# A four-block graph network on one core: x W1 between the counting windows, degrees from a column of ones, and the normalization moved from the matrix to rows and sums

## The reference

```python
ones = jnp.ones((src.shape[0],), x.dtype)
deg = jax.ops.segment_sum(ones, dst, num_segments=num_nodes) + 1.0
inv = jax.lax.rsqrt(deg)
h = x @ W
norm = inv[src] * inv[dst]
agg = jax.ops.segment_sum(h[src] * norm[:, None], dst, num_segments=num_nodes)
agg = agg + h * (inv * inv)[:, None]
return agg + b                       # then relu
```

## Time and profile before

| what | value |
|---|---|
| median of 3 runs | 5089.91 us |
| profiled execution | 5089.79 us |
| its span | 5087.7 us |
| TensorE busy in the span | 4957.9 us |
| counting | from 18.4 to 310.9 us |
| from the last count's copy to the first matmul of convolution 1 | 311.6 to 375.2 us |
| convolution 1, transposes, x W2, convolution 2, GRU inputs | 375.2 to 694.7 us |
| GRU and the three later blocks | from 698.9 us on |

### The profile page before, as it was taken

The page is one execution under the profiler, slowest core; times in us unless marked ns, Lnnn a source line. Parts: engine busy times, 40 slices in busy tenths (PEclk is TensorE's granted clock), DMA queues, the critical chain, the costliest instruction groups (busy, mean ns, idle before and its releaser), DMA issues.

```text
span 5087.7 us, 337016 instructions
## 1 busy us (share of the span) xinstructions
PE 4957.9 (97%) x131794; PEld 4250.1 (84%) x131795; DVE 2880.4 (57%) x16350; ACT 1950.7 (38%) x15372; POOL 846.6 (17%) x5071
## 2 busy tenths in 40 slices
PE   7899999999999999999999999999999999999989
PEld 7765579999999999999999999999999445555554
DVE  6551346666666666666666666666666525445551
ACT  0111025555555555555555555555555101222110
POOL 0000012222222222222222222222222000000000
PEclk9999999999999999999999999999999998999989
DMA  1011210000000000000000000000000100011011
GB/s 61 0 70 68 102 38 0 0 0 0 0 0 0 0 0 0 0 0 0 0 0 0 0 0 0 0 0 0 0 0 0 59 17 19 18 36 36 22 51 42
DMA packets 28932, 81.11 MB, mean 16 GB/s; under 512 B 1594, under 2 KB 1834, under 8 KB 28858
## 3 DMA queue, kind: packets, MB, share of 16 engines
q1 hardware_dynamic: 28858, 80.03, 4.3%
HBM read 58.08 MB, written 21.95 MB: 16 GB/s over the span
## 4 chain that ended last, share of the span: by engine, by line
PE 94%; DVE 2%; issue 2%; DVEq 1%; ACT 0%; POOL 0%; DMA 0%; ACTq 0%; SPq 0%; POOLq 0%
PE psum L494 64%; PE psum L567 8%; PE psum L363 5%; PE psum L353 4%; PE psum L579 4%; PE psum L411 3%; PE psum L476 2%; PE psum L553 2%; PE psum L643 2%; DVE r L880 1%; PE psum L426 0%; PE psum L458 0%; DVEq L875 0%; DVE r L879 0%; DVE stat L813 0%
## 5 line engine op out<-in xcount | busy, mean ns | idle before, releaser
L494 PE MATMUL psum<-h,r 128*128 128x16 f16 (+1 forms) x80000 | 3063.3, 181 | 9.1 <-ACT psum L707 4.3
L494 PEld LDWEIGHTS psum<-h,r 128*128 128x128 f16 x80000 | 2670.6, 96 | 39.1 <-DVEq L993 4.9
L494 PE MATMUL psum<-h,hn 128*128 128x16 f16 (+1 forms) x40000 | 2122.2, 177 | 0.0
L494 PEld LDWEIGHTS psum<-h,hn 128*128 128x128 f16 x40000 | 1592.6, 96 | 0.0
L999 DVE TENSOR_TENSOR_SCAN psum<-mul_rz,psum 128x6 f32<-128x6 f32 x5000 | 854.9, 171 | 590.8 <-PE psum L494 542.5
L707 ACT COPY psum<-big 128x2 f32 (+1 forms) x7506 | 1002.8, 163 | 0.0
L315 POOL TENSOR_TENSOR upd_add<-upd,signs 128x4 f32<-128x4 f32 x2500 | 504.2, 202 | 2591.2 <-DVE upd L1018 1832.0
L720 ACT ACTIVATE mul_n<-psum 128x2 f32<-128x2 f32 x2500 | 434.4, 174 | 1177.9 <-DVE psum L999 1177.8
L1018 DVE TENSOR_TENSOR_SCAN upd<-upd_mul,upd_add 128x8 f32<-128x8 f32 x2500 | 417.2, 167 | 300.4 <-ACT upd_mul L725 300.4
L729 ACT ACTIVATE upd_add<-psum 128x2 f32<-128x2 f32 x2500 | 434.1, 174 | 297.4 <-DVE psum L1005 297.4
L1014 DVE TENSOR_TENSOR_SCAN h<-upd_mul,upd_add 128x8 f16<-128x8 f32 x2500 | 425.2, 170 | 169.9 <-POOL upd_add L315 3.8
(11 more groups left out here) (224 smaller groups left out, 2538.1 us busy)
## 6 DMA issues: line engine op xcount, KB each, us to landing
ws<-in_Wl SPq DMA_DIRECT2D x9, 1024.0 KB, 5.4
ws<-in_Wr SPq DMA_DIRECT2D x9, 1024.0 KB, 7.6
edge_counts<-adj SPq DMA_DIRECT2D x2, 3051.8 KB
edge_weights<-big SPq DMA_DIRECT2D x1, 6103.5 KB
adj_rows<-big SPq DMA_DIRECT2D x1, 6103.5 KB
adj<-adj_rows SPq DMA_DIRECT2D x1, 6103.5 KB
big<-edge_counts SPq DMA_DIRECT2D x1, 6103.5 KB
adj<-edge_weights SPq DMA_DIRECT2D x1, 6103.5 KB
```

Source lines behind the costliest of these rows:

```text
L494: m = mm(places, whh16[g][:, part, 2 * kc + k, (2 * c + j) * P:(2 * c + j + 1) * P], state.unsqueeze(1).broadcast_to([P, COPIES, 2 - part] ...
```

## The change

- **x W1 in the counting.** `h1_half` puts two of the four matmuls of one tile of x W1 before each window. In 24 windows (12 rounds, H1 = NW // 2) that is 12 products for 10 tiles: two are computed twice. ScalarE stages the tile's columns of `r1` in `x_stage`, and copies each product from PSUM bank 4 to `hn`. `rows_product("h1", ...)` is gone. Before the first window TensorE now waits for W1. The edge columns `e_col` and `w_part` move out of `hn`.
- **Degrees from a column of ones.** `src_hot` holds 1 in column 1250 and 0 in columns 1251 to 1253, and VectorE writes only 1250 columns. So partition 125 of the tenth tile of the counts is the number of edges of each column. The windows are copied with 128 partitions. Ten matmuls with one column of the identity turn that row to a column; the 30 matmuls with ones and the ten of L435 are gone. Ten matmuls spread 1/max(degree, 1), ten more spread the inverse root.
- **No norm pass.** VectorE adds 1 on the diagonal only. ScalarE multiplies the rows of x W1 by `inv_col` (in place) and those of x W2 as it copies them. VectorE multiplies each sum of the convolutions by `inv_row` (`scale_cols`), and only then ScalarE adds bias and relu in place (`shift_cols`). The copies of the transposes become multiplications by `inv_col` and `inv_row`.
- **The counts in five stores** of 250 columns each, each issued when its five windows are copied.

```diff
+            for q in range(NW // 5):
+                sp.wait_ge(s("win_counts"), 5 * q + 5)
+                columns = slice(5 * q * WD, (5 * q + 5) * WD)
+                sp.dma_start(tiles(d_cnt)[:, :, columns], adj_v[0:NP, :, columns]).then_inc(s(f"cnt_out{5 * q // (NW - 5)}"), 16)
...
+            def h1_half(i, u):
+                if u == 0:
+                    pe.wait_ge(s("x_staged"), i + 1)
+                    pe.wait_ge(s("h1_stored"), i + 1)
+                for k in range(2 * u, 2 * u + 2):
+                    m = mm(psum[0:NP, 4], x_stage[:, k], wslot(0)[:, k], start=(k == 0), stop=(k == KT - 1), skip_group_check=True)
+                if u == 1:
+                    m.then_inc(s("h1_done"), 1)
...
+            pe.wait_ge(s("w1_in"), 16)
+            with pe.Fori(0, H1) as i:
                 for u in range(2):
+                    h1_half(i, u)
                     window(2 * i + u, u)
...
             pe.wait_ge(s("win_counts"), NW)
+            for t in range(NT):
+                m = mm(psum[0:NP, 7, t:t + 1], adj_v[:, NT - 1, t * NP:(t + 1) * NP], ident[:, NP:NP + 1], start=True, stop=True, skip_group_check=True)
+            m.then_inc(s("deg"), 1)
+            pe.wait_ge(s("win_read"), NW + 2)
+            pe.wait_ge(s("h1_stored"), H1 + 1)
+            for b, (name, column) in enumerate((("invdeg_col_ready", invdeg_col), ("inv_col_ready", inv_col))):
+                pe.wait_ge(s(name), 1)
                 for t in range(NT):
+                    m = mm(psum[:, 4 * b + t // 4, (t % 4) * NP:(t % 4 + 1) * NP], column[0:NP, t:t + 1].to_broadcast([NP, P]), ident[0:NP, 0:NP],
+                           start=True, stop=True, skip_group_check=True)
+                m.then_inc(s("inv_rows"), 1)
+            pe.wait_ge(s("inv_rows_read"), 1)
+            agg_cols("conv1", 4, hn, adj_v, "scaled", first=lambda t: (pe.wait_ge(s("h1_scaled"), t + 1), pe.wait_ge(s("loops"), t + 1)))
...
+            with act.Fori(0, H1) as i:
+                take_window(2 * i, 0)
+                act.wait_ge(s("h1_done"), i + 1)
+                nc.scalar.copy(hn[0:NP, bass.ds(i * NT // H1, 1)].rearrange("p t n -> p (t n)"), psum[0:NP, 4]).then_inc(s("h1_stored"), 1)
+                stage((i + 1) % H1)
+                take_window(2 * i + 1, 1)
...
+            for t in range(NT):
+                nc.scalar.activation(hn[0:NP, t], hn[0:NP, t], ACT.Copy, scale=inv_col[0:NP, t:t + 1]).then_inc(s("h1_scaled"), 1)
             act.wait_ge(s("small_in"), 48)
+            shift_cols("conv1", r2, b1c)
+            take_rows("h2", 4, scale=inv_col)
+            shift_cols("conv2", r1, b2c)
...
+            dve.wait_ge(s("deg"), 1)
+            v.tensor_scalar(inv_col[0:NP], psum[0:NP, 7, 0:NT], 1.0, None, ALU.add).then_inc(s("deg1_col"), 1)
+            link(v.tensor_scalar(invdeg_col[0:NP], psum[0:NP, 7, 0:NT], 1.0, None, ALU.max))
+            link(v.reciprocal(invdeg_col[0:NP], invdeg_col[0:NP]))
+            dve.sem_inc(s("invdeg_col_ready"), 1)
+            for t in range(NT):
+                if t in (0, NT - 2):
+                    dve.wait_ge(s(f"cnt_out{t // (NT - 2)}"), (64, 16)[t // (NT - 2)])
+                diag = adj_v[0:NP, t, t * NP:(t + 1) * NP]
+                v.tensor_tensor(diag, diag, ident[0:NP, 0:NP], ALU.add).then_inc(s("loops"), 1)
+            for b, row_of in enumerate((invdeg_row, inv_row)):
+                dve.wait_ge(s("inv_rows"), b + 1)
+                for c in range(3):
+                    n0, n1 = 4 * NP * c, min(4 * NP * (c + 1), N)
+                    link(v.tensor_copy(row_of[:, n0:n1], psum[:, 4 * b + c, 0:n1 - n0]))
+                dve.sem_inc(s(("invdeg_ready", "inv_rows_read")[b]), 1)
             dve.wait_ge(s("x_in"), 16)
             dve.wait_ge(s("bfc_in"), 16)
             link(v.tensor_tensor(xr[0:NP], xr[0:NP], fc_bias[0:NP].unsqueeze(1).broadcast_to([NP, NT, D]), ALU.add))
+            def scale_cols(name, bank0, dst, i0, i1):
+                for i in range(i0, i1):
+                    n0, n1 = NCH[i % 3]
+                    dve.wait_ge(s(f"{name}_done"), i + 1)
+                    v.tensor_tensor(dst[:, i // 3, n0:n1], psum[:, bank0 + i % 4, 0:n1 - n0], inv_row[:, n0:n1], ALU.mult).then_inc(s(f"{name}_scaled"), 1)
+            scale_cols("conv1", 4, r2, 0, 12)
...
+                    v.scalar_tensor_tensor(out=wt_v[0:NP, d, 4 * q * NP:4 * q * NP + width], in0=psum[0:NP, n % 4, 0:width], scalar=inv_col[0:NP, d:d + 1],
+                                           in1=inv_row[0:NP, 4 * q * NP:4 * q * NP + width], op0=ALU.mult, op1=ALU.mult).then_inc(s("tr_stored"), 1)
+            scale_cols("conv2", 0, r1, 0, 4)
             dve.wait_ge(s("whh_in"), 48)
...
+            scale_cols("conv2", 0, r1, 4, 6)
...
             for g in range(2):
                 link(v.tensor_copy(ws[:, 0:WSLOT], whh[g]))
                 split(g, ws[:, 0:WSLOT])
+                scale_cols("conv2", 0, r1, 6 + 2 * g, 8 + 2 * g)
+            scale_cols("conv2", 0, r1, 10, 12)
             split(2, ws[:, WSLOT:2 * WSLOT])
```

More of the change, by code:

```diff
@@ L52 @@
 COPIES = 16
+H1 = NW // 2
 def layout(nc, io):
@@ L354, in rows_product, with agg_cols @@
                     m.then_inc(s(f"{name}_done"), 1)
-            def agg_cols(name, bank0, rows, mat):
+            def agg_cols(name, bank0, rows, mat, read="stored", first=None):
                 i = 0
@@ L360, in agg_cols @@
                     for n0, n1 in NCH:
-                        o = out_rows(i, bank0, None, f"{name}_stored")
+                        o = out_rows(i, bank0, None, f"{name}_{read}")
                         for t in range(NT):
+                            if first and i == 0:
+                                first(t)
                             m = mm(o[:, 0:n1 - n0], rows[0:NP, t, f * P:(f + 1) * P], mat[0:NP, t, n0:n1],
@@ L415, in window @@
                 m.then_inc(s("win_done"), 1)
-            with pe.Fori(0, NW // 2) as i:
+            pe.wait_ge(s("w1_in"), 16)
+            with pe.Fori(0, H1) as i:
                 for u in range(2):
+                    h1_half(i, u)
                     window(2 * i + u, u)
-            for w in range(NW // 2 * 2, NW):
+            for w in range(2 * H1, NW):
                 window(w, w % 2)
             pe.wait_ge(s("win_counts"), NW)
-            for c, (n0, n1) in enumerate(NCH):
-                for t in range(NT):
-                    m = mm(psum[:, 4 + c, 0:n1 - n0], ones[0:NP], adj_v[0:NP, t, n0:n1], start=(t == 0), stop=(t == NT - 1))
-                m.then_inc(s("deg"), 1)
@@ L428, in _ @@
[L428 to L445, removed]
@@ L662, in take_cols, with take_rows, shift_cols @@
                         i += 1
[L664 removed]
+            def take_rows(name, bank0, base=0, scale=None):
                 for t in range(NT):
                     act.wait_ge(s(f"{name}_done"), base + t + 1)
[L668 removed]
+                    if scale is None:
+                        m = nc.scalar.copy(hn[0:NP, t], psum[0:NP, bank0 + t % 4])
+                    else:
+                        m = nc.scalar.activation(hn[0:NP, t], psum[0:NP, bank0 + t % 4], ACT.Copy, scale=scale[0:NP, t:t + 1])
+                    m.then_inc(s(f"{name}_stored"), 1)
+            def shift_cols(name, dst, bias):
+                i = 0
+                for f in range(KT):
+                    for n0, n1 in NCH:
+                        act.wait_ge(s(f"{name}_scaled"), i + 1)
+                        nc.scalar.activation(dst[:, f, n0:n1], dst[:, f, n0:n1], ACT.Relu, bias=bias[:, f:f + 1]).then_inc(s(f"{name}_stored"), 1)
+                        i += 1
             def take_turned(name, bank0, to=r2):
```

72 lines of the change are left out of this document (21 added, 51 removed).

## The result

The changed kernel has a median of 5040.98 us over 4 runs (5035.88 to 5043.26). The kernel before has 5088.57 over 4 runs. The ratio is 0.9907, with a 95% interval of 0.9892 to 0.9922: 0.9% faster. The forecast was 5046, in a range of 5034 to 5066.

The account below looks back on a forecast made before the run. TensorE, busy 4957.9 of 5087.7 us, was taken as the bound, so what it does or waits for counts. Terms 6.9 - 8.6 - 45.1 + 1.9 + 0.65 + 0.5 = -43.7 took 5089.8 to 5046 us, range 5034 to 5066.

Parts of the forecast that it names:

- the counting: Counting up to the last counts' copy: boundaries, clock and start together, -1.7 us.
- the cold start: Start of convolution 1: after TensorE's idle time it begins at a slow clock, +1.9 us, bounds 0 and 2.
- the transposes: Transposes after convolution 1: copies become longer multiplications and begin later, +0.5 us, bounds 0 and 3.
- The path after the counting: From the last count's copy to convolution 1: 18.5 us, set by the fifth store, instead of 63.56, -45.1 us.
- Boundaries: Between counting windows: half-products of x W1 lengthen 23 boundaries by 0.3 us each, +6.9 us, bounds 0 and 39.8.
- Clock: In the counting: eight of ten stretches at 1.2 GHz vanish, -8.6 us, bounds 0 and -10.8.
- the first rival: In the counting: the slow stretches stay, so 8.6 us are missing, total 5055 us; chance 0.18.
- Start: Start of the counting: the first half-product ends before the first one-hots are there, 0 us, within 1.5 either way.
- The end of convolution 2: End of convolution 2: VectorE's scaling is added to the chain before the GRU products, +0.65 us.
- The second rival: At counting boundaries: register loads don't run under the half-products, 39.8 us in place of 6.9, total 5079; chance 0.06.
- the third: Fifth store: small pieces as slow as large ones, convolution 1 37 us later, total 5083 us; chance 0.05.
- the slower one: At counting boundaries: half-products run at 1.2 GHz and counting after them stays slow, +60 us, total 5108; chance 0.03.

Follow-up runs that it names:

- e1: The changed kernel with the counts stored in two pieces of five tiles after the counting, as before the change: 5078.62 us, ratio 0.9981.
- e4: The changed kernel with two more unread float32 matmuls of 512 columns at each of the 24 boundaries: 5078.14 us.
- e2: The kernel before, with two float32 matmuls of 512 columns, results thrown away, ahead of each of 24 windows: 5079.57 us, ratio 0.9984.
- e5: The changed kernel with x W1 after the counting again and nothing before the windows: 5069.99 us, ratio 0.9968.
- e7: The changed kernel with e3's order, last boundary filled, transposes before each tile of x W2, turned matrix stored in ten pieces: 5029.33 us; run again 5029.78.
- e3: The changed kernel with inv_row's three copies ahead of the wait for the fifth store and diagonals 8 and 9: 5035.81 us; run again 5036.25.
- e6: The changed kernel with the transposes copied plainly, without inverse roots: 5035.89 us.
- b0: The changed kernel unaltered, run again beside repeats of e3 and e7: 5037.18 us, ratio 0.9911.

## Why the prediction was right, and where its terms were off

By the spans, the kernel became 50.4 us faster where 43.7 were forecast. The mechanism was the one described. The largest miss is the counting, 6.2 us better than its term; the path after it was 0.5 better, the cold start and the transposes together 1.8 worse, and 1.9 us come from the part behind the convolutions, which no term covers and which varies by more than that between profiles of the same kernel.

**The path after the counting** was read rightly, and its term was nearly exact: -45.6 for -45.1. Its steps hold one by one, with one small error covered by another chain. The fifth store landed 13.6 us after T (14.0 forecast), so a piece of 1000 bytes took (13.6 - 1.5) / 250 = 48 ns, where 50 was taken between 44 and 56. By the rule of the Trainium skill, "DMA: Bandwidth & Descriptors", Specifications (line rate from 512 bytes on), the estimate was 40 ns, a fifth of a piece of 5000 bytes. The trace does not bear that out and lies between it and the edge loads' 56: a piece of 5000 bytes took 195 ns in e1 ((50.4 - 1.5) / 250), a fifth of which is 39, so the short piece costs a quarter more per byte. The 1.5 us of start and landing were worked out from the same stores; without them, e1's second store landed 24.4 us after the first, 195 ns for each of its 125 pieces per engine. The banks were full at +9.2 (8 forecast; the clock fell during L451, which the store covered). Behind the store came 0.5 and 2 x 1.84 us, as worked out.

**The counting** is the term that was mis-sized: -7.9 for -1.7.
- Boundaries: 1.90 and 2.18 us for what was forecast as 2.12. Against 1.78 and 1.94 before, this is 12 x 0.12 + 11 x 0.24 = +4.1; added up one by one from the two timelines, the 23 boundaries are 4.5 us longer, not 6.9. What filled the gap does run under the half-product; e4 shows that only the gap's length is free.
- Clock: all ten slow stretches are gone, where eight were taken. The ten windows in which they stood are 1.0 to 1.4 us shorter each, 11.6 together; the forecast had 8.6, and 10.8 as its bound, from a price of 1.08 each. e2 shows that the filling does it, and e5 that they come back without it. So the first rival falls. Its argument, that only ten of 24 gaps were followed by a stretch, was a fact about when they strike and no sign of another cause: in e5 they strike at other windows. How often a gap is followed by one is not fixed either: behind the last boundary, which stays unfilled in all kernels but e7, a slow stretch stands in four profiles (e2, e3, e6, b0) and in none of the other seven.
- Start: 0 was taken, within 1.5. The first window ends at 58.77 us where it ended at 59.50: -0.7. Its matmuls begin 0.3 later, behind the slow half-product (four records in 3.75 us, 18.9 to the end instead of 18.1), but the first 90 matmuls took 4.96 us before, while the first 132 take 5.43 now. This fits matmuls that are slow only for the first microseconds, a time which the half-product now takes up; it was not tested alone. The three parts add up: 4.5 - 11.6 - 0.7 = -7.8, against -7.9 measured.

**The cold start of convolution 1** was named as a cost and came: +2.6 for +1.9. With 2 us of idle time in front of it, the two profiles each of e3's order and of e7 don't have it (84.05 us), but e5, with the same 1.99 us, pays 1.7. So a shorter idle time made it rarer here; it did not rule it out.

**The transposes** cost +1.6 for +0.5. The duration of the multiplication was right (0.73 us in the trace for 0.74; a copy of 500 columns took 0.67), but the slack of four banks was taken to absorb it, and over 30 groups it does not: a queue that is drained slower than it is filled uses its slack once. e6 puts all of it on that operation.

**The end of convolution 2**: +0.66 for +0.65. The scalings between VectorE's reductions delay nothing, as forecast: it worked 13.9 us on the reductions, and TensorE took the same 84.22 us.

The second rival (register loads not overlapped) falls with the boundaries, the third (pieces as dear as large ones) with the store, and the slower one with both: no half-product after the first runs at 1.2 GHz.

## What to carry to other kernels

If TensorE idles for a microsecond or two at regular places, look at the granted clock behind each of them; work moved there can be free, and here it even bought time, up to the length of the gap and no further. When two chains meet at one start, cost both: here moving x W1 without cutting the store gave 8 us of the 46 (e1), and cutting the store without moving x W1 gave 17.6 (e5). And after such a change look at what is queued in order behind the new last wait: six copies, 3.7 us, stood behind a store that they don't need, and taking inv_row's three out from behind it let convolution 1 start 5.4 to 6.6 us earlier.

## What the runs showed of the hardware

Adding 41 us of matmuls whose results are thrown away made the kernel before 7.5 us faster (e2). At ten of 24 boundaries an idle gap of 1.1 to 1.6 us was followed by 3.4 us at 1.2 GHz, at places that move from kernel to kernel, at a cost of 1.0 to 1.4 us each. An idle time of 1.99 us in front of convolution 1 was followed by such a stretch in one profile (e5) and not in four others (two of e3's order, two of e7). The part of the program that is the same in every version took from 4380 to 4393 us in thirteen profiles, more than most of the single steps above: steps of a few microseconds can be read from the starts of the stages, and not from the total.
